# Evicting every second bank of the table stage on ScalarE, with the bias added by TensorE

## The reference, cut to what matters

```
qkv = jnp.einsum('bchw,oc->bohw', x, qkv_w) + qkv_b[None, :, None, None]
...
k = qkv[:, 1].reshape(b * HEADS, HD, eh, ew)
v = qkv[:, 2].reshape(b * HEADS, HD, eh, ew)
k_sel = _grid_sample_zeros(k, grid)
v_sel = _grid_sample_zeros(v, grid)
```

## Time and profile before

| | |
|---|---|
| median of 3 runs | 30578.0 us (30551.67 to 30579.78) |
| the profiled execution, its own time | 30593.57 us |
| its span in the trace | 30591.8 us |
| mean granted TensorE clock | 0.785 of full |
| PE, DVE, ACT, POOL busy | 67%, 61%, 41%, 56% |
| table stage, PE products (9216 records) | 2444.0 us busy |
| table stage, DVE evictions (4608) | 1658.1 us busy |
| table stage, ACT normalizations (144) | 301.8 us busy |

### The profile page before, as it was taken

The page is one execution under the profiler, slowest core; times in us unless marked ns, Lnnn a source line. Parts: engine busy times, 40 slices in busy tenths (PEclk is TensorE's granted clock), DMA queues, the critical chain, the costliest instruction groups (busy, mean ns, idle before and its releaser), DMA issues. The chain is left out here.

```text
span 30591.8 us, 334063 instructions
## 1 busy us (share of the span) xinstructions
PE 20497.2 (67%) x111180; PEld 16820.9 (55%) x111180; DVE 18746.2 (61%) x33423; ACT 12680.2 (41%) x31540; POOL 17139.7 (56%) x16423
## 2 busy tenths in 40 slices
PE   3676766767576756767667666766667675677767
PEld 3466545666366554665456553665546653565556
DVE  6775557654775557755676547755576546765542
ACT  0444434443444424444344434444344434444331
POOL 1774557645675557645675557755576456755300
PEclk8787877877788867887778877888678877788787
DMA  6562454525554444625545355634545255544524
GB/s 192 131 194 80 138 141 121 172 75 160 129 168 118 117 135 133 189 76 148 143 123 158 91 148 132 184 94 132 135 130 178 76 154 132 147 140 112 149 78 128
DMA packets 2315942, 4118.47 MB, mean 135 GB/s; under 512 B 558288, under 2 KB 1591888, under 8 KB 2165968
## 3 DMA queue, kind: packets, MB, share of 16 engines
q1 hardware_dynamic: 1789632, 3005.20, 33.2%
q0 software_dynamic: 524288, 1074.79, 14.1%
q10 hardware_dynamic: 272, 16.78, 0.2%
HBM read 2554.47 MB, written 1557.40 MB: 134 GB/s over the span
## 5 line engine op out<-in xcount | busy, mean ns | idle before, releaser
L1266 POOL DMA_INDIRECT at_G<-table,at_idxg x16384 | 17012.4, 1038 | 11134.1 <-DVE at_M L1412 5712.9
L1301 ACT ACTIVATE at_E<-at_S,at_mx 128x64 f32<-128x64 f32 x16384 | 4017.5, 336 | 855.2 <-DVE at_mx L1404 847.0
L1440 DVE SCALAR_TENSOR_TENSOR at_x<-kc_attention,kc_pb,at_x 128x256 f32<-128x256 f32 x1024 | 494.8, 483 | 4928.7 <-PE kc_attention L1377 4808.4
L1307 ACT ACTIVATE at_KM<-kc_attention,kc_headmask 128x256 f32<-128x256 f32 x4096 | 1604.1, 476 | 3022.3 <-PE kc_attention L1355 3020.1
L358 PE MATMUL kc_ring<-kc_wkv,tb_xn 128*128 128x256 f32 x9216 | 2444.0, 418 | 532.3 <-DVE tb_T L374 473.5
L867 PE MATMUL kc_ring<-kc_ident,pl_R 128*128 128x128 f32 x4608 | 1218.8, 415 | 2317.9 <-DVE pl_R L903 2317.9
L1347 PE MATMUL kc_attention<-at_vals,at_PT 128*128 128x68 f32 x16384 | 2252.0, 296 | 688.3 <-DVE at_S L1397 466.9
L1347 PEld LDWEIGHTS kc_attention<-at_vals,at_PT 128*128 128x128 f32 x16384 | 2206.2, 214 | 838.5 <-issue 455.7
L1368 PE MATMUL kc_attention<-at_KM,at_Qm 128*128 128x256 f32 x8192 | 2505.4, 460 | 131.5 <-ACT at_KM L1307 131.3
L1412 DVE TENSOR_TENSOR at_M<-at_G,at_wtsc 128x2048 f32<-128x2048 f32 x1024 | 2338.5, 2284 | 345.3 <-DMA at_G<-table,at_idxg 340.4
L358 PEld LDWEIGHTS kc_ring<-kc_wkv,tb_xn 128*128 128x128 f32 x9216 | 1863.8, 211 | 948.5 <-DVE tb_T L374 561.0
(11 more groups left out here) (227 smaller groups left out, 38531.6 us busy)
## 6 DMA issues: line engine op xcount, KB each, us to landing
table<-tb_T SPq DMA_DIRECT2D x2304, 256.0 KB
at_G<-table,at_idxg POOLq DMA_INDIRECT x16384
cv_xr<-x_padded SPq DMA_DIRECT2D x288, 640.0 KB, 8.5
st_x<-in_x SPq DMA_DIRECT2D x288, 512.0 KB, 6.8
tb_x<-in_x SPq DMA_DIRECT2D x288, 512.0 KB
x<-cv_x SPq DMA_DIRECT2D x288, 512.0 KB
dc_x<-x SPq DMA_DIRECT2D x576, 256.0 KB
x<-dc_x SPq DMA_DIRECT2D x576, 256.0 KB, 3.2
```

The lines of the kernel that those rows point to most:

```text
L1266: pool.indirect_dma_start(self.G[n % 2][:, i, :, :].rearrange("p a c -> p (a c)"), None, entries[i % HEADS], bass.IndirectOffsetOnAxis(ap= ...
L1301: last = act.activation(self.E[:, p, h, p2, :], self.S[:, p, h, p2, :], ACT.Exp, bias=self.mx[:, i:i + 1])
L1307: last = act.activation(self.KM[:, :, h, :], self.kt_ps.rearrange("p (w k) -> p w k", w=GP), ACT.Copy, scale=headmask[:, h:h + 1])
```

## The change

Every second bank of the table stage (odd i) is evicted by ACT. ACT's copy adds no bias that varies along the columns, so PE puts the bias into these banks itself: ahead of the bank's two products comes one product of a row of ones, 1 x 128, with the bias row repeated four times, 1 x 512, which covers the whole bank; the two products then accumulate on it. `ps_free` becomes two semaphores, one for each evicting engine; PE waits for the one whose engine evicts bank n - 3, and SP's stores wait for both. ACT's normalization of the next chunk is now emitted after the eviction of bank i = 9. A new constant, `bkv4`, is loaded with four DMAs.

```
-    ps_free = m.sem("ps_free")
+    ps_free = [m.sem(f"ps_free_{e}") for e in ("dve", "act")]
...
-                    sp.wait_ge(ps_free, (k - 1) * BANKS + (xh + 1) * ROWS)
+                    for e in range(2):
+                        sp.wait_ge(ps_free[e], ((k - 1) * BANKS + (xh + 1) * ROWS) // 2)
...
-        for k in range(NCH):
-            yield k - .4
+        def normal(k):
             act.wait_ge(x_loaded[k % 2], (k // 2 + 1) * 32)
             if k > 1:
                 act.wait_ge(ps_ready, (k - 1) * BANKS)
             act.activation(xn[:, k % 2, 0:CH], xt[:, k % 2, :], ACT.Identity, bias=aff[:, 1:2], scale=aff[:, 0:1]).then_inc(xn_ready, 1)
+
+        normal(0)
+        for k in range(NCH):
+            for i in range(1, BANKS, 2):
+                n, xh, r = k * BANKS + i, i // ROWS, i % ROWS
+                yield k + (i + .5) / BANKS
+                if r == 1 and k:
+                    act.wait_ge(t_stored[xh], k * (16 * 2 * HEADS))
+                act.wait_ge(ps_ready, n + 1)
+                for s in range(2):
+                    last = act.activation(T[:, xh, s, :, r, :, :].rearrange("p h x c -> p x h c"),
+                                          ring[:, n % RING, :].rearrange("p (x s h c) -> p s x h c", x=2, s=2, h=HEADS)[:, s], ACT.Copy)
+                last.then_inc(ps_free[1], 1)
+                if i == BANKS - 7 and k + 1 < NCH:
+                    normal(k + 1)
...
                 if n >= RING:
-                    pe.wait_ge(ps_free, n - RING + 1)
+                    pe.wait_ge(ps_free[(n - RING) % 2], (n - RING) // 2 + 1)
+                if n % 2:
+                    pe.matmul(ring[:, n % RING, :], c["ones"][0:1, :], c["bkv4"][0:1, :], start=True, stop=False)
                 for sh in range(2):
                     o = r * W + xh * P + sh
                     mm = pe.matmul(ring[:, n % RING, sh * 2 * P:(sh + 1) * 2 * P], xn[:, k % 2, o:o + P],
-                                   c["wkv"][:, :, :].rearrange("p s c -> p (s c)"), start=True, stop=True)
+                                   c["wkv"][:, :, :].rearrange("p s c -> p (s c)"), start=n % 2 == 0, stop=n % 2 == 0 or sh == 1)
...
-            for i in range(BANKS):
+            for i in range(0, BANKS, 2):
...
-                last.then_inc(ps_free, 1)
+                last.then_inc(ps_free[0], 1)
...
+ *[(c["bkv4"][0:1, a * P:(a + 1) * P], k["bkv"].rearrange("(a n) -> a n", a=1)) for a in range(4)],
```

More of the change, by code:

```diff
@@ L1457, in load_constants @@
     c = {n: h.sb(n, shape) for n, shape in (
-        ("wsel", [P, HEADS * 4, Q]), ("osb", [P, HEADS * 4]), ("wc", [P, 2]), ("base", [P, 2, NPAIR]), ("wkv", [P, 2, P]), ("bkv", [P, P]),
+        ("wsel", [P, HEADS * 4, Q]), ("osb", [P, HEADS * 4]), ("wc", [P, 2]), ("base", [P, 2, NPAIR]), ("wkv", [P, 2, P]), ("bkv", [P, P]), ("bkv4", [1, 4 * P]),
         ("wq", [P, P]), ("bqs", [P, 1]), ("pb", [P, 1]), ("headmask", [P, HEADS]), ("rel_bias", [P, HEADS, Q]), ("pw", [P, 2, C]), ("ident", [P, P]),
@@ L1486, in _ @@
             sp.wait_ge(zeroed, 1)
-            for dst, src in ((c["base"][:, :, :].rearrange("p a n -> p (a n)"), k["grid"]), (c["wc"][:, :], k["window_coord"]), (c["bkv"][:, :], row(k["bkv"], P)),
+            for dst, src in ((c["base"][:, :, :].rearrange("p a n -> p (a n)"), k["grid"]), (c["wc"][:, :], k["window_coord"]), (c["bkv"][:, :], row(k["bkv"], P)), *[(c["bkv4"][0:1, a * P:(a + 1) * P], k["bkv"].rearrange("(a n) -> a n", a=1)) for a in range(4)],
                              (c["wq"][:, :], k["wq"]), (c["bqs"][:, :], column(k["bq"])), (c["pb"][:, :], column(k["proj_b"])), (c["headmask"][:, :], k["headmask"]),
```

## The result

The changed kernel takes 31245.4 us (four runs, 31207.5 to 31282.9), the kernel before 30578.9: ratio 1.0219, 95% interval 1.0202 to 1.0237. That is +666 us; +390 was forecast, with 31300 as the upper end. The direction, the places and the engine were right, and the size was not.

The account below looks back on a forecast made before the run. PE and DVE taking turns, neither full, was taken to bound the kernel. Table stage beside attention +296, first table +92 and constants +2 made +390 us on 30578, so 30968 us; range 30700 to 31300.

Parts of the forecast that it names:

- My own sum with waits of 1 to 3 us: Whole kernel: the forecast itself, with PE waiting 1 to 3 us a group, 30830 to 31110 us; chance 0.50.
- the two slower rivals: Whole kernel: rival 1 at 31235 us, chance 0.20, and Rival 2 at 31292 us, chance 0.18.
- rival 1: Table stage: ACT's attention work delays its evictions, PE's idle stays 3.94 us, a group takes 29.8; 31235 us, chance 0.20.
- What bounds the kernel: Table stage beside attention: PE and DVE take turns, neither full; a group takes 25.8 us, PE idle 3.94 at full clock.
- the sum of 25.9 us against 25.8: Table stage: PE's work per group at full clock, 19.5 + 6.3 = 25.9 us, already as long as the whole group before.
- The price of the product: PE's new bias product in each changed bank: 0.87 us, between 0.52 and 1.18; 6.3 us more per group.
- forecast +92: First table, made alone ahead of the loop: PE becomes the limit, 5.8 us more for each of 16 chunks, +92 us.
- The waits that are left: Table stage: PE still waits 2.0 us a group, between 1.0 and 2.8, making the group 27.9 us; +296 us in all.
- waits gone altogether: Table stage: PE has no waits left, +0.1 us a group, total 30686 us; chance 0.05.
- ACT's side: ACT's two copies per changed bank: 0.39 us each, 5.7 us a group, hidden by PE; later exponentials cost nothing.
- Rival 2: Table stage: the granted clock stays at 0.90, a group takes 30.2 us; +620 us there, total 31292, chance 0.18.
- Rival 3: Table stage: product costs 0.52 us and fits PE's gaps, group 24.2; total 30403, sign turns near 0.68, chance 0.07.

Follow-up runs that it names:

- run 1: The changed kernel with the bias product contracting 128 rows (weights 1/128, bias row on all 128 partitions) instead of one: 30708.6 us, ratio 1.0040.
- run 3: The changed kernel without the bias product, so the odd banks that ACT evicts get no bias: 30273.3 us, ratio 0.9899.
- run 5: The changed kernel with the bias product in bf16, the bias row split into three parts on 32 partitions each, weights 1/32: 30325.9 us, ratio 0.9913.
- Run 6: The kernel of run 5 with the bf16 product contracting only the first 32 rows, leaving out two bias parts: 30471 us in a single execution.

## Why the prediction was right in sign and short in size

*The total*: 31245 lies in the range, and that is in part luck. My own sum with waits of 1 to 3 us ended at 31110. The range reached to 31300 for the two slower rivals; rival 1's 31235 is within 10 us of the result, and what it rests on did not happen (below).

*What bounds the kernel*: right. PE and DVE took turns, and more work on PE could only be paid from 3.9 us of idle time a group. PE is the limit after the change, as the sum of 25.9 us against 25.8 said.

*The price of the product*: the step that failed. I took 0.87 us between bounds of 0.52 and 1.18, "as the nearest row has its type and its columns and differs in the rows contracted alone". The rows contracted were the point: the product costs 1.25, outside even the upper bound, and 0.86 with 128 rows (run 1). What I had priced at nothing is the switch between products of 128 rows and one of fewer. In the first table this term alone makes 8 x 0.38 x 16 = 49 us, forecast +92 and measured +138; run 1 has +84.

*The waits that are left*: 2.0 us was too much. With the product at the price that I had assumed, run 1 has a group at 25.9 us, not 27.9: 24.9 of PE's busy time and 1.0 of waits. So the 25.9 were 1 us too high too. About half of that can be told: my 19.54 us of PE work counted three ends a group that stick out into idle time, 0.16 us each (a record lasts 0.379 where the next can start after 0.215), and they cost nothing once another product follows at once. The rest stays open. The two errors, 1.25 for 0.87 (+2.8) and 27.9 for 25.9 (-2.0), partly cancelled in the forecast of 27.9 against 29.0; the last 0.3 comes with a lower clock, 0.95 against 0.99 in run 1. Run 1's total, 30709, lies close to the 30686 that I gave to "waits gone altogether".

*ACT's side*: right. Its copies last 381 ns where 390 was taken, and the exponentials behind them hold nobody up: in the changed kernel's stretch PE waits in no row for ACT. Rival 1, ACT at the head of the line, is refuted beside the attention (PE waits 0.6 us a group for ACT's evictions even without a product), but its mechanism works in the first table, where I had looked at engine sums alone: 3 us a chunk in run 3, as much in run 5 (18.4 us where PE needs 15.5), hidden in the changed kernel by PE.

*Rival 2, the clock*: in between, 0.95. PE filled the gaps, and in the groups of the stretch where it did so entirely the clock is 1.00. Behind a wait of about 2 us the lower level can still follow, and groups like that of 33.78 us pay for it. The Trainium skill's rule on waits between bursts (TensorE: Matmul & The Clock Gate, HAM oscillation — how this bites in real kernels) agrees in direction. Run 1 has the same waits and keeps the full clock (last section).

*Rival 3, the price at which the sign turns*: I put it at 0.68 us. Against the kernel before on the same chip the runs have -129 us at 0.52 and +120 at 0.86, so on a straight line it lies near 0.70. Run 6 has the very price of this rival, 0.52: I computed a group of 24.2 us and 30403 for it, measured are 24.4 and 30471, with 11 us of the difference at the start. The rule that the weight loads' share shows how full PE is (the Trainium skill, Perfetto Trace Analysis, Identifying the Most-Contended Engine) fails here: that share is 63% in the changed kernel's stretch (314.58 of 499.42), and PE stands idle for 13 us of it; the measurement decides.

| product | price, us | group, us | total, us |
|---|---|---|---|
| none | 0 | 23.1 | 30273 |
| bf16, 128 rows | 0.21 | 23.5 | 30326 |
| bf16, 32 rows (single execution) | 0.52 | 24.4 | 30471 |
| fp32, 128 rows | 0.86 | 25.9 | 30709 |
| fp32, 1 row | 1.25 | 29.0 | 31245 |

7.27 products a group: the first 0.2 us of price (1.5 us of work a group) cost 0.4 us of time, since PE still waits there, and the last 0.39 are paid in full, 2.8 us of work and, with the lower clock, 3.1 of time.

## What to carry to other kernels

Where two engines take turns, moving work off one pays only what the other has room for; price what the move adds to the other before counting the gain. Here a bias entered through the accumulation for 0.21 us a bank, once its product had the 128 rows of its neighbours (padded, with weights that make up for the repetition) and was split into bf16 parts. And before work is put on an idle engine, look at what that engine waits for: its waits cost nothing only as long as nobody stands behind them.

## What the runs showed of the hardware that I had not expected

Among products of 128 rows, a product of 1 or 64 rows in fp32 lost 0.39 us, and one of 32 rows in bf16 0.3. At the switch to it and at the switch back, the weight load starts with its product instead of one ahead. With 128 rows nothing is lost, between fp32 and bf16 neither. Between the two records of one fp32 product, which have the same few rows, the second load is in time: as far as that goes, the loss comes with the change of the number of rows. A longer row of products with few rows was not tried, and which part of TensorE causes the loss no run here tells.

A short wait can be followed by a lower clock for much longer than it lasts. The timeline of PE in the changed kernel, behind a wait of 1.95 us for the division:

```profile
9364.77 0.44 PE L1377 MATMUL kc_attention<-kc_ident,at_att 128*128 128x128 f32 x2 [1.95 <-DVE at_att L1450]
9365.14 1.92 PE L372 MATMUL kc_ring<-kc_bkv,kc_ones 1*128 1x512 f32 x2
9366.99 3.78 PE L375 MATMUL kc_ring<-kc_wkv,tb_xn 128*128 128x256 f32 x8
```

and the busy time and granted clock (the third number from the end) of the 10 us behind the wait and of 10 us after:

```profile
9365.10:9375.30 10.20, 10.20 (x19) 5.53 (x19) 0.76 (x2) 1.97 (x7) 7.62 (x8) 0.51 0.42 118
9376.00:9386.00 10.00, 10.00 (x48) 6.76 (x47) 7.72 (x15) 2.43 (x7) 2.20 (x3) 1.00 0.62 147
```

Eight table records take 3.78 us at the level of 1.2 GHz and 1.99 at 2.4, while PE is busy throughout. Behind this wait of 2 us about 5 more were lost.

The wait alone does not do it. In run 1, where the product has 128 rows, the same wait is followed by the full clock, as the timeline and the 10 us behind it show:

```profile
9080.52 0.44 PE L1377 MATMUL kc_attention<-kc_ident,at_att 128*128 128x128 f32 x2 [2.02 <-DVE at_att L1450]
9080.80 1.02 PE L372 MATMUL kc_ring<-kc_bkv,kc_rowmean 128*128 128x512 f32 x2
```

```profile
9080.70:9090.70 10.00, 10.00 (x47) 7.34 (x47) 1.90 (x5) 1.60 (x5) 7.56 (x9) 1.00 1.00 304
```

Counted in groups 53 to 68 of each of the eight pieces, 32 waits of PE last 1.7 to 2.6 us in the changed kernel, and behind 21 of them the lower level begins within 3 us; with 64 rows behind 20 of 32, with 128 rows behind none of 32. So part of what the one-row product costs beside the attention is clock: 5% of the time in these groups is spent at the lower level, with 128 rows none. What in the product makes the difference the runs don't show.
